# A two-part graph network: the dense edges' scatters in node order, 108 of them moved into layer 1, and half of a raw pair's rounding moved to VectorE

## The reference

```python
h = relu(layernorm(x))
for i in range(3):                                    # first network, "layers 1 to 3" here
    msg = relu(h[src]) + 1e-7
    ex = exp(msg - max over the edges of each dst)
    out = segment_sum(msg * ex, dst) / segment_sum(ex, dst) + h
    t = out @ W1[i] + b1[i]
    t = relu((t - t.mean(0)) * rsqrt(t.var(0) + 1e-5) * gamma[i] + beta[i])
    h = relu(t @ W2[i] + b2[i])
x = x + h
# second network: three layers over nodes and edges, with edge_attr (64) and the same src, dst
out = x + second(relu(layernorm(x)), edge_attr)
```

## Time and profile before

| | us |
|---|---|
| median of three runs | 4170.22 |
| lowest and highest | 4170.03, 4172.24 |
| the profiled execution, its own time | 4165.19 |
| its span | 4163.4 |
| PE busy in the span | 3299.3 (79%) |
| POOL (GpSimd) busy | 2373.3 (57%) |
| DVE (VectorE) busy | 2217.1 (53%) |
| ACT (ScalarE) busy | 1941.5 (47%) |

### The profile page before, as it was taken

The page is one execution under the profiler, slowest core; times in us unless marked ns, Lnnn a source line. Parts: engine busy times, 40 slices in busy tenths (PEclk is TensorE's granted clock), DMA queues, the critical chain, the costliest instruction groups (busy, mean ns, idle before and its releaser), DMA issues.

```text
span 4163.4 us, 70803 instructions
## 1 busy us (share of the span) xinstructions
PE 3299.3 (79%) x19961; PEld 2595.9 (62%) x19961; DVE 2217.1 (53%) x5689; ACT 1941.5 (47%) x3697; POOL 2373.3 (57%) x2488
## 2 busy tenths in 40 slices
PE   2287777769898789888699888758788888888887
PEld 0144444458777677777577777746666666666665
DVE  6144333325444555445665445736666666666666
ACT  0222111146555576555585555734444444444444
POOL 2666666646666366666356665255565565565552
PEclk6588988889999899999899999879999999998988
DMA  7155433467777367777367776554444444444442
GB/s 291 54 184 191 138 119 120 124 202 246 248 235 236 117 231 234 251 234 242 110 230 243 243 235 197 151 160 126 124 129 129 127 128 128 128 125 127 127 125 63
DMA packets 419116, 713.14 MB, mean 171 GB/s; under 512 B 75585, under 2 KB 259067, under 8 KB 416098
## 3 DMA queue, kind: packets, MB, share of 16 engines
q0 software_dynamic: 130688, 321.08, 26.0%
q1 hardware_dynamic: 270119, 323.45, 25.5%
q10 hardware_dynamic: 18107, 66.24, 4.2%
HBM read 561.11 MB, written 149.39 MB: 171 GB/s over the span
## 4 chain that ended last, share of the span: by engine, by line
PE 36%; another core or an unknown queue 18%; issue 14%; DVE 14%; ACT 10%; DVEq 2%; ACTq 2%; DMA 1%; SPq 1%; POOL 0%; POOLq 0%
PE ps L1570 17%; PE ps L1593 4%; ACT casts L1466 2%; PE ps L718 2%; DVE acc L2369 2%; DVE acc L2403 2%; PE ps L2242 2%; DVE onehot L2396 1%; PE ps L2221 1%; ACTq L934 1%; DVE acc L2396 1%; PE ps L712 1%; ACT two_parts L1456 1%; PE ps L700 1%
## 5 line engine op out<-in xcount | busy, mean ns | idle before, releaser
L2211 POOL DMA_INDIRECT ring<-h_table,idx_ring x832 | 815.9, 981 | 563.2 <-issue 272.9
L652 POOL DMA_INDIRECT pair_rings<-split_table,src_idx x728 | 713.6, 980 | 409.8 <-issue 202.5
L1570 PE MATMUL ps<-casts,two_parts 128*128 128x500 f32 (+1 forms) x3464 | 823.1, 391 | 141.4 <-DVE two_parts L1660 73.8
L1570 PEld LDWEIGHTS ps<-casts,two_parts 128*128 128x128 f32 x3464 | 646.3, 198 | 280.2 <-DVE two_parts L1660 83.5
L665 POOL DMA_INDIRECT adjacency<-acc x508 | 495.8, 976 | 344.4 <-issue 144.7
L1660 DVE TENSOR_TENSOR two_parts<-work,two_parts 128x512 fp32r<-128x512 f32 (+1 forms) x276 | 187.4, 679 | 588.9 <-ACT two_parts L1456 349.8
L1466 ACT ACTIVATE casts<-spare 128x1000 fp32r<-128x1000 fp8e4 (+1 forms) x471 | 458.9, 974 | 8.5 <-PE ps L1570 4.8
L2308 ACT ACTIVATE work<-acc,vecs 128x512 f32<-128x512 f32 x208 | 150.2, 722 | 562.4 <-DVE acc L2369 303.5
L1456 ACT ACTIVATE two_parts<-work 128x512 fp32r<-128x512 f32 (+1 forms) x276 | 169.7, 615 | 452.8 <-remote 232.5
L2221 PE MATMUL ps<-ident,ring 128*128 128x128 f32 x1664 | 292.3, 298 | 83.6 <-issue 59.2
L2260 PEld LDWEIGHTS ps<-mats,work 128*128 128x128 f32 x1664 | 238.2, 204 | 141.7 <-issue 140.4
(11 more groups left out here) (333 smaller groups left out, 6242.6 us busy)
## 6 DMA issues: line engine op xcount, KB each, us to landing
spare<-adjacency SPq DMA_DIRECT2D x216, 250.0 KB
acc<-e_few SPq DMA_DIRECT2D x208, 256.0 KB
work<-msg_table SPq DMA_DIRECT2D x144, 256.0 KB
work<-in_edge_attr SPq DMA_DIRECT2D x104, 256.0 KB
e_few<-spare SPq DMA_DIRECT2D x52, 512.0 KB
spare<-rel_rows SPq DMA_DIRECT2D x208, 84.0 KB
spare<-adjacency SPq DMA_DIRECT2D x72, 187.5 KB
e_few<-work SPq DMA_DIRECT2D x26, 512.0 KB
```

What stands on the lines that cost most here:

```text
L652: e.indirect_dma_start(out=to, out_offset=None, in_=table, in_offset=bass.IndirectOffsetOnAxis(ap=src_idx[:, 2 * i + h, j:j + 1], axis=0)) ...
L1570: ins = e.matmul(bank, parts_of(d)[:, b % 2, q, kind * D:(kind + 1) * D], cast_counts[n % CASTS][:, at:at + width], start=opens, stop=(b = ...
L2211: e.indirect_dma_start(out=rows[:, s, j, :], out_offset=None, in_=h_table, in_offset=bass.IndirectOffsetOnAxis(ap=idx_ring[:, s, j:j + 1], ...
```

## The change

Three things are edited together.

1. The dense edges are laid out in four segments of 127 columns. Column c of segment s holds edges of the s-th quarter of the dense edges, so that the scatters now go through the nodes in order. The search for repeated edges works on four pieces of 127 + 78 columns in place of one of 508 + 78. Of the clears only those of regions 0 and 1 stand ahead of the loads of x on ScalarE's queue; those of regions 2 and 3 stand behind them, and the first scatter waits for the first six, the 128th for the others.
2. Of the 508 scatters 400 (`EARLY`) stay in the setup phase; 108 are issued by GpSimd in the edges phase of layer 1, ahead of its gathers, and wait for no attribute pair. In layer 1 the loops get 15 more steps ahead of step 0 (`LEAD`), which hold the first 75 blocks (`LEAD_BLOCKS`; all are 1000 wide), 5 in each; the other 121 are spread evenly over the 42 steps of the pairs. SyncE waits for the end of all scatters ahead of its first load of region 2.
3. In a raw pair of layers 2 and 3 the high part of the first half is made by VectorE (a `tensor_copy`), that of the second half by ScalarE as before.

```diff
+SEGMENTS = 4
+WIDE = COLS // SEGMENTS
+REACH = WIDE + 2 * NEAR
+EARLY = 400
+LEAD = 15
+LEAD_BLOCKS = 75
...
-def step_of(n):
+def step_of(layer, n):
     r, b = divmod(n, BLOCKS)
+    columns = [sum(widths) for _, widths in REGIONS]
+    before = sum(BLOCKS * w for w in columns[0:r]) + b * columns[r]
+    if layer == 0:
+        lead = sum(columns[k // BLOCKS] for k in range(LEAD_BLOCKS))
+        if n < LEAD_BLOCKS:
+            return n * LEAD // LEAD_BLOCKS - LEAD
+        return (before - lead) * PAIRS // (BLOCKS * sum(columns) - lead)
     if r == 0:
         return b * FIRST_STEPS // BLOCKS
...
-        def scatters(e, S):
-            e.wait_ge(S("zero_fill"), 16 * FILLS * len(REGIONS))
-            e.wait_ge(S("addresses"), 1)
-            for i in range(COLS):
+        def scatters(e, S, first, end):
+            for i in range(first, end):
                 n = i // EACH
+                if i == 0:
+                    e.wait_ge(S("zero_fill"), 16 * FILLS * 2)
+                if i == WIDE:
+                    e.wait_ge(S("zero_fill_rest"), 16 * (FILLS * (len(REGIONS) - 2) + 1))
                 if i % EACH == 0 and n >= SCATTERS:
                     e.wait_ge(S(f"gather_spread{n % SCATTERS}"), 16 * EACH * (n // SCATTERS))
-                if i % EACH == 0:
+                if i % EACH == 0 and i < EARLY:
                     reached(e, S("few_e0"), 2 * pairs_behind(n))
...
-                scatters(e, S)
-                scattered(e, S)
+                e.wait_ge(S("addresses"), 1)
+                scatters(e, S, 0, EARLY)
+                scattered(e, S, EARLY)
...
+                    for r in range(2):
+                        clear(r)
                 for k in range(5):
                     at = slice(k * PART, (k + 1) * PART)
                     by_sixteens(e, x_rows[:, at, :], a["x"][:, k * PART * D:(k + 1) * PART * D].rearrange("p (t d) -> p t d", d=D), S(f"x{k}"))
+                if not again:
+                    for r in range(2, len(REGIONS)):
+                        clear(r)
...
+                    if ready and d == 2 * DUOS:
+                        scattered(e, S, COLS)
...
             def pool(e, S):
+                if ready:
+                    scatters(e, S, EARLY, COLS)
                 for i in range(PAIRS):
...
-                for i in range(-1, PAIRS + 3):
+                for i in range(-lead - 1, PAIRS + 3):
...
                         for h in range(2):
                             exp_of_pair(i, h)
-                        for h in range(2):
-                            high_of_pair(i, h)
+                        high_of_pair(i, 1)
...
+                def high_of_first_half(i):
+                    parts = half_slots[2 * slot_of(i)]
+                    e.wait_ge(S("p_mul"), 2 * i + 1)
+                    e.tensor_copy(parts[:, :, 0, :], half_values[2 * slot_of(i)][:, :, 1, :]).then_inc(S("p_high0"), 1)
```

More of the change, by code:

```diff
@@ L83, in chunks_before, with blocks_halfway @@
     return sum(len(widths) for _, widths in REGIONS[0:r])
-def step_of(n):
+def step_of(layer, n):
     r, b = divmod(n, BLOCKS)
+    columns = [sum(widths) for _, widths in REGIONS]
[5 more added lines that the diff above has]
+        return (before - lead) * PAIRS // (BLOCKS * sum(columns) - lead)
     if r == 0:
         return b * FIRST_STEPS // BLOCKS
[L91 to L98, removed]
+    first = BLOCKS * columns[0]
+    return FIRST_STEPS + (before - first) * (PAIRS - FIRST_STEPS) // (BLOCKS * sum(columns) - first)
+def blocks_halfway(layer, i):
+    steps = [step_of(layer, n) for n in range(BLOCKS * len(REGIONS))]
     return sum(s < i for s in steps) + sum(s == i for s in steps) // 2 if i in steps else 0
@@ L922, in act, with clear @@
             def act(e, S):
+                def clear(r):
+                    width = PITCH if sum(REGIONS[r][1]) > PITCH // 8 * 7 else sum(REGIONS[r][1])
+                    rows = adjacency[r * SPAN * PITCH:r * SPAN * PITCH + NR * PITCH, :].rearrange("(p b d) o -> p b (d o)", b=BLOCKS, d=PITCH)
+                    for h in range(FILLS):
+                        at = slice(h * BLOCKS // FILLS, (h + 1) * BLOCKS // FILLS)
+                        n = at.stop - at.start
+                        zeros = Z0[:, 0:-(-n * width // 4)].bitcast(U8)[:, 0:n * width].rearrange("p (b d) -> p b d", d=width)
+                        e.dma_start(rows[:, at, 0:width], zeros).then_inc(S("zero_fill" if r < 2 else "zero_fill_rest"), 16)
                 if not again:
@@ L1295, in edges_phase @@
             columns = iota_w[:, :]
+            lead = LEAD if ready else 0
+            JOBS = JOBS_OF[layer]
             by_node = [work[0:WW, b, 0:2 * D] for b in range(2)]
@@ L1341, in duos_at @@
             def duos_at(i):
-                return [d for d in range(ALL_DUOS) if step_of(first_block(d)) == i + 1]
+                return [d for d in range(ALL_DUOS) if step_of(layer, first_block(d)) == i + 1]
             def blocks_of(u):
@@ L1355, in evacuated @@
             def evacuated(i):
-                return [r for r in range(len(REGIONS)) if step_of(BLOCKS * (r + 1) - 1) + 1 == i]
+                return [r for r in range(len(REGIONS)) if step_of(layer, BLOCKS * (r + 1) - 1) + 1 == i]
             def jobs_of(i):
@@ L1596, in sum_pair @@
                     ins.then_inc(S("sums"), 1)
-                for i in range(PAIRS + 3):
-                    blocks = [n for n in range(ALL_BLOCKS) if step_of(n) == i]
+                for i in range(-lead, PAIRS + 3):
+                    blocks = [n for n in range(ALL_BLOCKS) if step_of(layer, n) == i]
                     first = 1 if 0 <= i - 1 < raw else 0
```

116 lines of the change are left out of this document (59 added, 57 removed).

## The result

| | us |
|---|---|
| before, median of 4 runs | 4171.23 |
| changed, median of 4 runs (lowest, highest) | 4316.09 (4304.09, 4324.6) |
| ratio changed / before, 95% interval | 1.033 (1.027 to 1.038) |
| the profiled execution, its own time and its span | 4304.09, 4302.3 |

The ratio is one of means: the change makes the kernel 3.3% slower. By the medians it is +145 us, from one profiled execution to the other +139 us (span 4163.4 to 4302.3). The forecast was +87.

A forecast was written before the change was run, and what follows sets the result against it. GpSimd's indirect DMAs and TensorE's matmuls were taken to share the time, neither at its own pace. -20 - 163 + 103 + 171 - 4 = +87 on 4165.2 gives 4252, plus 5 to the median: 4257 us; range 4118 to 4315.

The forecast's parts named there:

- (a): Setup phase: first scatter at about 54 instead of 73.8, so free scatters end 20 us earlier; -20 us (bounds -10, -25).
- (b): Setup phase: 316 scatters follow from 203.5 on instead of 424; 108 fewer at 1.51 us each, -163 us.
- (c): Setup phase: attribute pairs don't shrink, 28 are left behind the last scatter; 24 more at 4.31 us, +103 us (bound +116).
- attribute pairs stay slow: Rival, setup phase: attribute pairs don't speed up when scatters stop; +54 us, 4311 us in all, chance 0.08.
- the early start doesn't come: Rival, setup phase: x or the clears are late, so the earlier first scatter is lost; +20 us, 4277 us, chance 0.04.
- (d): Layer 1's lead: scatters end at +136, TensorE does 20 of 75 blocks by then; lead ends at +241 (bounds +165, +257).
- the slow regime: After some eight unbroken indirect DMAs on GpSimd other engines hardly move, until it pauses; 1.2 matmuls per us taken in the lead.
- lead interleaved: Rival, layer 1: lead loses only 0.036 us per matmul, ends near +165, pairs take 11.6 us; 4182 us, chance 0.13.
- (e): Layer 1's pairs: 11.6 us a step, first sum at +245, last at +721; layer 1 gets 171 us longer.
- (f): Layer 1: SyncE's new wait ahead of region 2's counts comes after the scatters are over; costs nothing.
- +12 without a cover: Raw pairs, layers 2 and 3: VectorE copies hold gathers back 1 us each if GpSimd's waits don't hide it; +12 for -4.
- rival without a slow regime: Layer 1: TensorE isn't held up by GpSimd's unbroken issue; lead ends at +165, pairs 10.2 us; -46, 4124 us, chance 0.25.

## Why the prediction was wrong in size and right in sign

The forecast was 4257 us and the range ended at 4315; the median is 4316.09. The prediction had added its bad ends to +160, which from 4170 is 4330, so the range was drawn tighter than its own sum. By parts the measured change is -75 + 223 - 9. No term stands for the -9 of the final phases; they don't differ between the kernels, so it is chance, and it hides a part of the miss in the profiled execution.

**(a), (b), (c), the setup phase: right.** Predicted -20 - 163 + 103 = -80, measured -75. The first scatter is at 53.9 (predicted 54). Behind the pause 316 scatters take 662.73 - 185.16 = 477.6 us, 1.51 us each, as in the earlier trace rows. From the last scatter to the last attribute matmul it is 119.7 us where it was 13: +107 for +103, at 694.86 - 690.55 = 4.31 us a pair. The start moved by 18 to 20, which is the prediction's -20. So the rival "attribute pairs stay slow" and the rival "the early start doesn't come" are out.

**(d), the lead: right in kind, 41 us too small.** GpSimd's side came as forecast: the scatters end at +137.2 (predicted +136), four gathers follow, and the wait for block 72. TensorE's side did not. I took 1.2 matmuls per us from the stretch with the most work; the lead had 80 matmuls, 10 blocks in place of 20, and that is worth 10 x 1.82 = 18 us. I let the stalls end with GpSimd's pause; they went on for some 15 us after it, 946 against 931, in which two blocks were done: 12 us. The rest, 9 us, is behind the stalls. I reckoned 75 blocks ahead of the first sum, but it stands behind the three blocks of step 0 as well: 66 blocks from 946.32 to the sum at 1074.02, 127.7 us, where 63 x 1.82 and 4 us make 118.7. The last 1 us is GpSimd's. The step that failed is "I take 1.2", and with it that the stalls end with GpSimd's pause; even the bound at 0.5 matmuls per us, +257 for the 75 blocks, was 22 us short of the +279 at which they were done. A rate of matmuls was the wrong unit. The lead advances by a block or two per hand-over between engines, and it is the hand-over that takes up to 42 us. The prediction also had the slow regime set in after "some eight DMAs" and end when GpSimd pauses. In the lead six blocks came through beside the first 32 scatters, and the stalls outlasted the last gather by 15 us. The rival "lead interleaved", with the lead over near +165, is out on chip A.

**(e), the pairs: 12 us too small.** Predicted 11.6 us a step, measured (1561.36 - 1074.02) / 41 = 11.9, so 487 in place of 476. The number is near, but the reason given for it, 0.036 us per matmul, was not tested: on chip B steps with 2.9 and 4.3 blocks differ by 0.2 us. Layer 1 was forecast at +171 and took +223: 41 from (d), 12 from (e).

**(f) and the raw pairs.** The wait for the scatters ahead of region 2 is nowhere seen; they had landed long before. The raw rounding was forecast at -4 and is worth nothing that can be told, 1.001 (0.999 to 1.003). The +12 without a cover would be 1.003, the very end of the interval. Two readings were off: a copy took 0.80 us (L1673), not 1.2, and the steps take 97.8 / 7 = 14.0 us on average, not the 13.2 of the first one. The Trainium skill ("SBUF — State Buffer", Who interferes with whom) has VectorE's copies in a two-port mode and GpSimd shut each other out; here 16 more copies cost nothing that can be told, and whether they ran in that mode no run shows.

**The rival without a slow regime is real, on another chip.** Its numbers were a first sum at +170, pairs at 10.2 us, the last sum at +588, and -46 us. On chip D the two kernels with the whole move show +167 and +169, 10.4 and 10.3, +595 and +589, and 54 and 59 us less than the kernel before. They differ from the change in five pauses and in one wait, and the change itself was not run on D. I had counted this rival as a doubt about the mechanism. It turned out to hold on one chip of four: the other three show the slow regime. The Trainium skill ("Runtime: NRT & Kernel Launch", Instruction fetch mechanics) has the fetching of instructions in straight code hidden, and chip D looks so. Whether late instructions are what stalls A, B and C, no run shows; in the second stop of the lead no packet of an instruction queue moves, which speaks against it. I had also taken 0.036 us per matmul as a law between GpSimd and TensorE. On D gathers in the final phases take 600 / 462 = 1.30 us each beside 10.2 matmuls, where that line gives 1.63, so it too is a price of the slow chips.

## What to carry over

A long run of indirect DMAs that waits for nobody is no free work: on three of four chips it stopped the other engines, and a move that makes such a run longer pays for it there. Six small memsets on GpSimd ahead of every eighth DMA cure it (chips B and C), and they pay where GpSimd would wait anyway: 12.7 us in the setup phase on chip C. Before you trust a rate read from one stall, look at what the engines hand to each other in it, and time the kernel before on more than one chip. The change costs 3.3 and 3.5% on chips A and C, and two near variants of it gain 1.5 and 1.7% on chip D, in one run each.

## What was unexpected of the hardware

- The same program takes 4171, 4223, 4216 and 3570 us on four chips. Instructions last the same wherever rows were compared; on D the hand-overs between them are short. Why is not known: no run varied anything but the program on a given chip, and chips B, C and D were each used at one time only.
- Where the stalls occur, they follow a grid. ScalarE resumes at 845.42, 890.21 and 935.00, 44.8 us apart, while GpSimd issues every 1.27 us, and VectorE's small instructions come 1.40 us apart (chip C). The stalls outlast GpSimd's last issue by some 15 us, as if something had to be worked off. What it is stays open; the DMA engines were busy for 0.15 of the lead and for 0.02 inside the second stop, so it is not packets that wait for them.
- A pause of 2.2 us is enough if it comes every 12 us (chips B and C), and it can be work of GpSimd's own.
